# First attention: keys of two key tiles in one PSUM bank, their values in another

## What is computed

```python
kv_dca = (y_dca @ Wkv_dca + bkv_dca).reshape(b, DCA, 2, H, HD)
k_dca = _ln(kv_dca[:, :, 0], kn_dca_w, kn_dca_b)
...
q = _ln((x @ Wq + bq).reshape(b, s1, H, HD), qn_w, qn_b)
kv = jnp.concatenate([y_main @ Wk + bk, y_main @ Wv + bv], axis=-1)
...
k = _ln(kv[..., :HD], kn_w, kn_b)
...
ctx = _attn(qT, k.transpose(0, 2, 1, 3), v.transpose(0, 2, 1, 3))
...
ctx_dca = _attn(qT, k_dca.transpose(0, 2, 1, 3), v_dca.transpose(0, 2, 1, 3))
ctx = ctx.transpose(0, 2, 1, 3).reshape(b, s1, QDIM)
...
ctx = ctx + DCA_WEIGHT * ctx_dca
return ctx @ Wo + bo
```

## Time and profile before

| | |
|---|---|
| times of three runs | 1566.47, 1570.98, 1572.76 us (median 1570.98) |
| span of the profiled execution, first to last instruction | 1569.8 us |
| TensorE | 1391.4 us busy (89%) |
| VectorE | 1242.9 us (79%) |
| ScalarE | 1106.1 us (70%) |
| GpSimd | 781.2 us (50%) |
| value copies L1763, 52 of them | 18.9 us busy, ScalarE idle ahead of them 48.1 us, for VectorE's L1458 |
| key adds L1458, 56 of them | 23.4 us busy, VectorE idle ahead of them 36.3 us, for TensorE |

### The profile page before, as it was taken

One profiled execution on the slowest core, in us unless ns is written; L12 is line 12 of the kernel. 1 busy time (PEld: TensorE's weight loads), 2 busy tenths in 40 slices (PEclk: granted clock), 3 DMA queues, 4 the chain that ended last, 5 costly groups with the idle time before them and its releaser, 6 DMA issues.

```text
span 1569.8 us, 25759 instructions
## 1 busy us (share of the span) xinstructions
PE 1391.4 (89%) x8524; PEld 685.8 (44%) x8524; DVE 1242.9 (79%) x2331; ACT 1106.1 (70%) x2028; POOL 781.2 (50%) x664
## 2 busy tenths in 40 slices
PE   5688888888887889789889989899999999999999
PEld 4243343343333244234445544455454445454545
DVE  6666767677587445769898988989899899999887
ACT  4656756764864665568688888778887787887764
POOL 4014014113203013238677668887697777676763
PEclk9798898998898999899999999999999999999999
DMA  4000300200242010010000000000010000000000
GB/s 165 1 1 28 59 1 1 53 12 1 43 129 83 2 54 1 6 43 22 6 1 1 1 22 22 7 1 22 1 28 1 28 3 26 10 18 1 1 1 28
DMA packets 20491, 36.71 MB, mean 23 GB/s; under 512 B 4898, under 2 KB 15238, under 8 KB 19334
## 3 DMA queue, kind: packets, MB, share of 16 engines
q1 hardware_dynamic: 20358, 35.07, 7.7%
HBM read 26.53 MB, written 1.15 MB: 18 GB/s over the span
## 4 chain that ended last, share of the span: by engine, by line
PE 34%; DVE 9%; issue 7%; POOL 4%; ACT 3%; DMA 0%; DVEq 0%; ACTq 0%; POOLq 0%
PE BK L713 33%; DVE arena L1694 5%; POOL arena L2090 3%; DVE arena L1675 2%; ACT arena L1952 1%; DVE arena L1708 1%; ACT arena L1963 1%; ACT arena L1945 1%; DVE arena L2278 0%; POOL arena L1085 0%; DMA arena<-in_wup 0%; POOL arena L2087 0%; DVE arena L998 0%; ACT L1945 0%; DVE arena L2284 0%
## 5 line engine op out<-in xcount | busy, mean ns | idle before, releaser
L713 PE MATMUL BK<-arena 128*128 128x512 bf16 (+12 forms) x8194 | 1345.1, 367 | 141.8 <-DVE arena L1512 38.6
L713 PEld LDWEIGHTS BK<-arena 128*128 128x128 bf16 (+6 forms) x8194 | 648.8, 111 | 808.5 <-issue 175.9
L2090 POOL TENSOR_TENSOR arena<-arena 128x512 f32<-128x512 f32 (+1 forms) x352 | 507.5, 1442 | 135.3 <-ACT arena L1945 110.8
L1694 DVE TENSOR_TENSOR arena<-arena 128x512 bf16<-128x512 f32 (+1 forms) x416 | 488.0, 1176 | 30.3 <-ACT arena L1952 29.5
L1945 ACT ACTIVATE arena<-BK,arena 128x512 f32<-128x512 f32 (+1 forms) x416 | 286.2, 688 | 130.1 <-PE BK L713 111.3
L1843 ACT ACTIVATE arena<-BK 128x512 f32<-128x512 f32 (+1 forms) x416 | 227.2, 603 | 90.1 <-PE BK L713 84.5
L1512 DVE TENSOR_REDUCE arena<-BK 128x1 f32<-128x512 f32 x384 | 244.3, 683 | 57.8 <-PE BK L713 56.4
L1952 ACT CAST arena<-arena 128x512 bf16<-128x512 f32 (+1 forms) x416 | 253.6, 610 | 0.0
L1675 DVE CUSTOM_DVE_ANT_0 arena<-BK,arena 128x512 bf16<-128x512 f32 (+1 forms) x256 | 145.1, 567 | 22.1 <-PE BK L713 19.2
L1963 ACT ACTIVATE arena<-BK 128x512 bf16<-128x512 f32 (+1 forms) x256 | 129.5, 508 | 41.3 <-PE BK L713 41.3
L2001 POOL TENSOR_TENSOR arena<-arena 128x256 f32<-128x256 f32 (+6 forms) x45 | 30.2, 671 | 184.7 <-ACT arena L1780 182.3
(11 more groups left out here) (177 smaller groups left out, 854.7 us busy)
## 6 DMA issues: line engine op xcount, KB each, us to landing
arena<-arena SPq DMA_DIRECT2D x144, 50.0 KB, 2.2
arena<-in_ctxT SPq DMA_DIRECT2D x8, 800.5 KB, 4.3
arena<-in_ctxk SPq DMA_DIRECT2D x4, 768.0 KB
arena<-in_wo SPq DMA_DIRECT2D x1, 2048.0 KB, 7.6
arena<-in_wqT SPq DMA_DIRECT2D x1, 2048.0 KB, 7.7
arena<-in_x SPq DMA_DIRECT2D x4, 256.0 KB, 9.7
arena<-in_rsel SPq DMA_DIRECT2D x1, 1024.0 KB, 9.4
arena<-in_rw1T SPq DMA_DIRECT2D x1, 1024.0 KB, 5.2
```

The costliest lines, as they stand in the source:

```text
L713: return T.matmul(out_, lhsT, rhs, start=start, stop=stop, skip_group_check=True)
L1694: V.tensor_tensor(Pl[k][0:m, :], P1[k][0:m, :], Ph[k][0:m, :], ALU.subtract).then_inc(p_low, 1)
L2090: G.tensor_tensor(acc[0:m, g % 2, :], acc[0:m, g % 2, :], P1[k][0:m, :], ALU.add).then_inc(summed1, 1)
```

## The change

The first 12 key tiles of each batch go in pairs `kp` = 0 to 5. Piece `kk(b, kp)` writes the keys of tiles 2kp and 2kp+1 to the two halves of one bank, `vv(b, kp)` their values to those of another. VectorE adds the bias to a whole `kk` bank in one instruction and frees it; ScalarE copies a whole `vv` bank in one and frees it, without waiting for VectorE. Both pieces stand where the even tile stood, and the place of the odd tile is empty; all yields stay. Tiles 12 and 13 stay as they were. Products and bank fills are as many as before.

```diff
@@ first_batch @@
-                piece("kv", 0, kt, bank=bank())
+                if kt >= 12:
+                    piece("kv", 0, kt, bank=bank())
+                elif kt % 2 == 0:
+                    piece("kk", 0, kt // 2, bank=bank())
+                    piece("vv", 0, kt // 2, bank=bank())
@@ prep @@
-                piece("kv", b, kt, bank=bank())
+                if kt >= 12:
+                    piece("kv", b, kt, bank=bank())
+                elif kt % 2 == 0:
+                    piece("kk", b, kt // 2, bank=bank())
+                    piece("vv", b, kt // 2, bank=bank())
@@ tensor_main @@
+                elif kind in ("kk", "vv"):
+                    b, kp = arg
+                    pe.wait_ge(ld_ctx[b], 16)
+                    pe.wait_ge(wk_centred, 1) if kind == "kk" else pe.wait_ge(ld_wv, 16)
+                    for k in range(2):
+                        k0 = 256 * kp + 128 * k
+                        t = mm(BK[i][:, 256 * k:256 * k + 256], ctxT[:, b % 2, k0:k0 + 128],
+                               (wk if kind == "kk" else wv)[:, 0, :])
+                    t.then_inc(full[i], 1)
@@ vector_main @@
-                    if b:
-                        dve.wait_ge(*filled("kt", b - 1, 1, 3))
...
+                elif kind == "kk":
+                    b, kp = arg
+                    dve.wait_ge(full[i], n + 1)
+                    dve.wait_ge(wk_centred, 2)
+                    if b:
+                        dve.wait_ge(*filled("kt", b - 1, 1, 3))
+                    V.tensor_tensor(kc[:, 2 * kp:2 * kp + 2, :], BK[i][:, :].rearrange("p (k n) -> p k n", k=2),
+                                    wk[:, 4, :].unsqueeze(1).to_broadcast([128, 2, D]), ALU.add).then_inc(free[i], 1)
@@ scalar_main @@
-                    m = 128 if kt < 12 else TMAIN
-                    act.wait_ge(va_ones, 6)
-                    act.wait_ge(p_used, 52 * (b - 2) + 40 + kt)
-                    act.wait_ge(k_done, 14 * b + kt + 1)
-                    A.copy(va[b % 2][0:m, kt, :, 0:16], heads(BK[i][0:m, 256:512])).then_inc(free[i], 1)
+                    m = TMAIN
+                    act.wait_ge(p_used, 52 * (b - 2) + 40 + kt)
+                    act.wait_ge(k_done, 2 * b + 1)
+                    A.copy(va[b % 2][0:m, kt, :, 0:16], heads(BK[i][0:m, 256:512])).then_inc(free[i], 1)
+                elif kind == "vv":
+                    b, kp = arg
+                    act.wait_ge(full[i], n + 1)
+                    act.wait_ge(va_ones, 6)
+                    act.wait_ge(p_used, 52 * (b - 2) + 40 + 2 * kp + 1)
+                    A.copy(va[b % 2][:, 2 * kp:2 * kp + 2, :, 0:16],
+                           BK[i][:, :].rearrange("p (k h d) -> p k h d", k=2, d=16)).then_inc(free[i], 1)
...
-                        act.wait_ge(k_done, 14 * b + min(hi, 14))
+                        act.wait_ge(k_done, 2 * b + 2) if j == 3 else act.wait_ge(*emptied("kk", b, hi // 2 - 1))
@@ sync_main @@
-                    sp.wait_ge(k_done, 14 * B)
+                    sp.wait_ge(k_done, 2 * B)
```

## The result

| | before | after |
|---|---|---|
| median of the runs, same chip | 1569.03 us (11 runs, 1563.70 to 1577.36) | 1561.88 us (11 runs, 1557.68 to 1565.96) |
| span of the profiled execution | 1569.8 us | 1564.6 us |
| TensorE's granted clock in it | 0.957 | 0.957 |
| TensorE, VectorE, ScalarE busy | 1391.4, 1242.9, 1106.1 us | 1390.6, 1242.7, 1104.2 us |

The ratio is 0.9958 (95% interval 0.9938 to 0.9978). The means of all three comparisons, weighted by their scatter, give 0.9967 (0.9958 to 0.9977), that is 5.1 us less. The forecast was 1566.1 us in a range of 1559 to 1574, 4.85 us off the span; the two profiled spans lie 5.2 us apart at the same mean clock. The first comparison's 7.15 us was on the high side.

What follows compares the result with a forecast made beforehand. TensorE, busy 89% of the span, was taken as the bound, so only its waits counted. Terms 0.7 + 0.95 + 0.5 + 2.2 + 0.5 = 4.85 us off 1569.8 give 1565.0; the median lies 1.2 above: 1566.1 us, range 1559 to 1574.

Steps and rivals of the forecast that it cites:

- Merged work at nothing: Key adds and value copies: merging saves 3.8 us of VectorE and 3.7 us of ScalarE, costed at nothing on the path.
- Start, 0.7 us: Start of batch 0: earlier cast and no wait for `wv` give 0.7 us, bounds 0.3 and 1.1.
- the cast comes 0.27 us earlier: Start of batch 0: tile 3's copy needs the bank alone, so ScalarE's cast starts at 14.94 us, 0.27 us earlier.
- Batch 1, 1.45 us: Batch 1: the 0.95 us wait for exponentials goes, and 0.5 us of a 1.85 us wait for bank 7's copy.
- the first rival: Handed on: a shift gained in one batch is eaten by the next wait; time 1571 us, chance 0.17.
- Batch 2, 2.2 us: Batch 2: the query gets bank 3 and waits of 2.87 us go; 2.2 us taken, bounds 0 and 2.87.
- Batch 3, 0.5 us: Batch 3: the query waits for bank 7, but a 1.37 us wait goes; net 0.5 us, bounds -0.86 and 1.37.
- Emptied steps at nothing: Eight steps in batches 1 to 3 lose their odd tile's 0.86 us product; costed at nothing, since idle shares are alike.
- if the first attention ends less than 2 or more than 9 us earlier: End of the first attention: a shift outside 2 to 9 us earlier would show the forecast wrong.
- Emptied steps cost: Rival: eight steps lose their 0.86 us cover, 6.9 us less the 4.85 gained; 1573 us, chance 0.07.
- the clock of the tile stretches falls: Rival: TensorE's granted clock in the key-tile stretches drops from 0.983 to 0.875, 13.8 us more; 1580 us, chance 0.04.
- More goes: Rival: half of the 14.0 us idleness remaining in the three key-tile stretches goes too; 7 us more, 1559 us, chance 0.18.

Runs made afterwards that it cites:

- e2_split: The change with each pair's key add and value copy taken apart again into two instructions of 256 columns; 1559.64 us, ratio 0.9971.
- r_before: The kernel before, unchanged, run once more for one execution with a second trace; no time of its own is given.
- e1_order: The kernel before with both tiles of a pair at the even one's place, each keeping its own add, wait and copy; 1563.55 us, ratio 0.9994.
- e3_wait: The change with each pair's value copy waiting for the same pair's key add again; 1561.6 us, ratio 0.994.
- r_after: The change, unchanged, run a second time against the kernel before, with a second trace; ratio 0.9973.
- e7_spread: The change with the bank counter set back at each batch and `vv` moved to the odd tile's place; 1563.2 us, ratio 0.9976.

## Why the prediction was right

The time and the sum came out (4.85 us forecast, 5.2 between the spans, 5.1 with an interval of 3.6 to 6.6 over three comparisons). The mechanism was right: nothing from the merged work, most from waits that the order and the banks remove. Its terms came out less well.

- **Merged work at nothing: right.** `e2_split` gives back 7.6 us of it and idles as the change does. The plain rows of 512 columns served (0.687 forecast and measured; 0.590 and 0.584). The estimate of 0.392 and 0.658 us that the prediction drew from the Trainium skill, "VectorE: DVE Perf Modes", section on the TRN2 errata, was under both: 0.414 to 0.422 and 0.687 us were measured.
- **Start, 0.7 us: not shown.** The profile of after has the cast at 13.96 us, 1.25 us earlier than in the earlier trace rows, and the wait for `wv` is gone. But `r_before` has it at 14.16, so most of that was scatter of the first loads. The first exponential starts at 89.91 and 89.17 us in the two traces of before and at 89.14, 87.50 and 87.25 in the three of the change. The means differ by 1.6 us, with scatter of the same size within one kernel. `e1_order` and `e3_wait`, where the copy waits for VectorE as before, cast at 13.96 and 13.94 us, no later than the change (13.96, 14.60 and 14.30). So the step by which the cast comes 0.27 us earlier because the copy is free is not borne out. Nor does the cast set the first exponential here: `r_after` casts latest of the three and starts its exponentials 1.64 us before the trace of after. One thing did move that the prediction doesn't have, ScalarE's table load, which stood behind the wait for the first add and now is done early, before and after:

```profile
10.80 1.28 ACT L1763 ACT_TABLE_LOAD   x1 [10.80 <-DVE arena L1458]
```

```profile
2.48 1.28 ACT L1791 ACT_TABLE_LOAD   x1 [2.48 <-POOL arena L2008]
```

  In `e3_wait` it is late again, at 10.77 us, and the cast at 13.94 is none the later. What limits the cast next is seen in `e7_spread`:

```profile
14.25 1.90 ACT L1806 CAST arena<-arena 128x2048 bf16<-128x2048 f32 x1 [0.48 <-DMA arena<-in_rsel]
```

- **Batch 1, 1.45 us: measured 1.06 us of idleness, 1.4 us of length at full clock.** The timeline of after, where the earlier trace rows had 1.85 us of waiting and copies behind VectorE:

```profile
105.58 0.61 ACT L1020 COPY arena<-BK 128x512 f32<-128x512 f32 x1
106.24 1.99 PE L721 MATMUL BK<-arena 128*128 128x256 f32 x8 [1.25 <-ACT arena L1020]
...
111.62 0.58 ACT L1791 COPY arena<-BK 128x512 f32<-128x512 f32 x1 [1.78 <-PE BK L721]
112.11 1.06 ACT L1809 ACTIVATE arena<-arena 128x1024 f32<-128x1024 f32 x1
```

  The 1.85 us are 1.25, a gain of 0.6 where 0.5 was taken, and the 0.95 us for exponentials are 0.2. The waits for maxima grew from 1.0 to 1.4 us, and the balance is 1.06 us: some of it was handed on, as the first rival had it.
- **Batch 2, 2.2 us: measured 1.5 us of idleness, 1.2 us of length at full clock (37.72 to 36.52 in steps 52 to 65).** The banks moved as read, and TensorE runs through the query without waiting:

```profile
222.94 6.68 PE L721 MATMUL BK<-arena 128*128 128x256 f32 x52
...
229.16 1.08 ACT L1872 ACTIVATE arena<-BK 128x512 f32<-128x512 f32 x2 [1.69 <-PE BK L721]
...
230.33 0.17 DVE L1548 TENSOR_REDUCE arena<-arena 128x8 f32<-128x32 f32 x1
...
230.65 0.27 PE L1222 MATMUL BK<-arena 128*16 128x128 f32 x1 [1.03 <-DVE arena L1548]
```

  What was forecast as late next, `mneg` behind VectorE's maximum, is late by 1.03 us. The term that was too large is "the scores of step 59, [...] come 2.2 us earlier": it sized the gain at the end of `mneg` and left out what the maxima behind it would take back. TensorE's waits for L1535 are 2.5 us in steps 52 to 65, those for L1512 2.0 before.
- **Batch 3, 0.5 us: 0.17 us less idleness, but 0.35 us more length.** "One wait of near 1.5 us in batch 3" was 1.72, and the 1.37 us for exponentials went. At full clock steps 104 to 117 grew (38.67 to 39.02 us): here the net sign of the forecast was wrong, and the gain of batch 3 comes from the steps before, in the next point.
- **Emptied steps at nothing: they cost nothing, but they bring something.** This is the missing term. The prediction argued from equal idle shares, and so priced neither a loss nor a gain; it compared stretches at a clock of 0.98 with stretches at 0.87, while step 101 alone, with its tile, was idle for 0.57 of 3.12 us. Steps 91 to 104 are 0.70 us shorter in all three traces of the change; steps 39 to 52, the same place a batch earlier, took 26.18 us before and 25.49 after at a clock of 1.00 (in the repeats 25.50 for the change at 1.00, and more wherever the clock was lower: 27.47 at 0.90). That makes 1.4 us, part of it (0.33 us each) by the order alone.

Measured terms together, as lengths at full clock: 1.4, 1.2 and -0.35 us and 1.4 us of the two stretches are 3.6 us, where the forecast without its start has 4.15. What lies between 3.6 and the 5.1 us of the times can be the start or scatter; the interval of 3.6 to 6.6 holds both. The terms of batches 2 and 3 were too large by 1.9 us together, and the missing one was 1.4 us: that the sum came so near is luck in part. The prediction's sign of being wrong, "if the first attention ends less than 2 or more than 9 us earlier" can't be judged: the last exponential starts at 557.3 and 556.0 us in the two traces of before and at 552.2, 556.4 and 549.6 in those of the change.

Of the rivals, "handed on" holds in part in each batch. "Emptied steps cost" and "the clock of the tile stretches falls" fell: the three stretches had 0.93, 0.93 and 1.00 before and 1.00, 0.95 and 1.00 after. The rule on cycling banks in the Trainium skill, "TensorE: Matmul & The Clock Gate", section on psum-queue depth-cycling, which would have made the clock rival likelier, is not borne out by these. "More goes" did not come: the most that any kernel here took away is 5.8 us of idleness, by other banks.

## What to carry to other kernels

Where engines work down one fixed list, ask first which piece stands ahead of which and which bank it has, and price the merged instructions last: making 24 adds and 24 copies out of 48 each was worth nothing that shows in the time, two products ahead of an output projection and another bank for the query most of it. A counter that runs on over batches deals banks by chance, and one line that sets it back took 3 us of waits away. To judge so small a change, compare equal steps where both traces have the same granted clock: these lengths repeated to 0.02 us, while times scatter by ten. TensorE's idleness repeated to 0.25 us, but in batch 3 it fell where the steps grew.

## What the runs showed of the chip

Executions of one kernel differ by the clock that TensorE is granted, and that is most of their scatter. In steps 117 to 130, which the change hardly touches, the kernel before in its two traces:

```profile
377.37:413.26 35.89, 30.64 (x233) 11.43 (x236) 22.38 (x45) 21.83 (x41) 12.41 (x9) 0.71 0.07 14
```

```profile
378.37:409.55 31.18, 24.63 (x232) 9.87 (x236) 22.07 (x45) 21.76 (x42) 12.43 (x9) 0.95 0.06 11
```

With the same work it took 4.7 us more at 0.71 than at 0.95, about the whole effect of the change. Over the 191 timed executions of the runs behind the first comparison whose mean clock is listed, a fit with one level for each version and one for each chip gives 10.6 us more for each 0.01 of clock less, with 2.8 us of scatter left. At equal clock the fit puts the change 2.7 us under the kernel before (standard error 0.7), `e1_order` 2.9 (1.0) and the version with reset banks 6.9 (0.7), so 4.3 (0.9) under the change. That agrees with the lengths at full clock (3.6 us for the change, 3.4 more for the reset) better than the medians do, though a fit is no experiment: whether a kernel with fewer waits also gets a different clock was not tried.
